# Gathers of a selective scan: 24 to 32 of a block's 64 taken from VectorE to ScalarE and GpSimd, with a convolution tap, an affine step and sums

## What is computed

```python
h = relu(adj @ x @ gcn_w + gcn_b)
h = (h - mu) * rsqrt(var + EPS) * ln_g + ln_b
xc, z = split(h @ w_in)
xconv = sum(xpad[k:k + L] * conv_w[:, k] for k in range(4)) + conv_b
u = silu(xconv)
dbc = u @ w_xp                       # 16 columns for dt, 16 for B, 16 for C
dt = softplus(dbc[:, :16] @ w_dt + b_dt)
hst = exp(dt * A) * hst + dt * B * u   # in time order, 512 channels x 16 states
ys = hst @ Ct
y = (ys + u * D_skip) * silu(z)
x = x + y @ w_out
```

## Time and profile before

| what | value |
|---|---|
| median of 3 runs (lowest, highest) | 2886.9 us (2885.34, 2891.23) |
| the profiled execution | 2887.87 us, span 2885.8 us |
| busy in the span | PE 87%, DVE 73%, ACT 47%, POOL 33% |
| chain that ended last | PE 51%, DVE 27%, issue 14%, ACT 6%, POOL 1% |
| mean granted TensorE clock | 0.937 of 2.4 GHz |
| first and last scan starts | 1336.7 and 2601.3 us |

### The profile page before, as it was taken

How to read it: one execution, slowest core, us unless ns; L and a number is a source line. 1 busy time by engine, 2 the same in 40 slices (tenths; PEclk the granted TensorE clock), 3 DMA queues, 4 the chain that set the end, 5 groups by cost and what they waited for, 6 DMA issues and landing times.

```text
span 2885.8 us, 24290 instructions
## 1 busy us (share of the span) xinstructions
PE 2505.6 (87%) x8262; PEld 1277.1 (44%) x8262; DVE 2119.0 (73%) x2426; ACT 1348.4 (47%) x1935; POOL 961.7 (33%) x723
## 2 busy tenths in 40 slices
PE   7998999999999999988888888888888876765997
PEld 3443444444444444443434343434434343443775
DVE  4665666666667664326999899999999999895564
ACT  4565656565646553214444434434353444552332
POOL 0002232313131313304455554645455464670000
PEclk9998999999999999999999999998999978777999
DMA  4222222222222231123323232322323110102021
GB/s 177 91 88 66 66 83 65 79 71 71 77 73 68 71 104 43 51 83 111 94 83 103 73 109 73 102 80 88 99 84 105 56 50 16 51 31 95 30 66 37
DMA packets 68412, 221.03 MB, mean 77 GB/s; under 512 B 7570, under 2 KB 7826, under 8 KB 67906
## 3 DMA queue, kind: packets, MB, share of 16 engines
q1 hardware_dynamic: 64082, 204.00, 22.4%
q0 software_dynamic: 3664, 14.45, 1.3%
q10 hardware_dynamic: 544, 1.05, 0.1%
HBM read 199.28 MB, written 20.19 MB: 76 GB/s over the span
## 4 chain that ended last, share of the span: by engine, by line
PE 51%; DVE 27%; issue 14%; ACT 6%; POOL 1%; DMA 1%; DVEq 0%; SPq 0%; ACTq 0%; POOLq 0%
PE ps L535 13%; DVE h L1265 9%; DVE acc L1239 7%; PE ps L558 5%; ACT th L1432 2%; PE ps L807 2%; PE ps L654 2%; PE ps L686 2%; PE ps L585 2%; PE ps L587 1%; PE ps L621 1%; PE ps L638 1%; PE ps L643 1%; DVE u L1182 1%; DVE wgt L966 1%
## 5 line engine op out<-in xcount | busy, mean ns | idle before, releaser
L1935 POOL TENSOR_TENSOR dB<-du,bc 128x512 f32<-128x512 f32 x512 | 649.3, 1273 | 559.2 <-DVE h L1265 556.4
L1265 DVE TENSOR_TENSOR_SCAN h<-ps,hst,dB 128x512 f32<-128x512 f32 x512 | 649.3, 1273 | 13.7 <-POOL dB L1935 6.6
L1432 ACT ACTIVATE ps<-dt,cols 128x512 f32<-128x512 f32 x512 | 350.9, 688 | 442.5 <-DVE h L1265 438.3
L535 PE MATMUL ps<-wgt,msg 128*128 128x512 f32 x1024 | 530.7, 621 | 23.0 <-DVE wgt L971 22.6
L558 PE MATMUL ps<-raw,msg 128*128 128x512 f32 x1024 | 543.4, 623 | 3.0 <-DMA msg<-tmp_m 3.0
L807 PE MATMUL ps<-consts,h 128*128 128x128 f32 x2048 | 353.5, 302 | 211.2 <-DVE acc L1239 196.9
L807 PEld LDWEIGHTS ps<-consts,h 128*128 128x128 f32 x2048 | 263.2, 153 | 531.9 <-DVE acc L1239 368.1
L1239 DVE SCALAR_TENSOR_TENSOR acc<-ps,Ct,acc 128x512 f32<-128x512 f32 x450 | 326.7, 726 | 8.9 <-PE ps L807 8.9
L535 PEld LDWEIGHTS ps<-wgt,msg 128*128 128x128 f32 x1024 | 184.2, 194 | 254.8 <-issue 200.7
L1432 ACT ACTIVATE wgt<-wgt 128x1024 f32<-128x1024 f32 x256 | 258.1, 1047 | 38.2 <-DVE wgt L966 35.7
L558 PEld LDWEIGHTS ps<-raw,msg 128*128 128x128 f32 x1024 | 176.5, 199 | 127.8 <-issue 127.0
(11 more groups left out here) (273 smaller groups left out, 3682.9 us busy)
## 6 DMA issues: line engine op xcount, KB each, us to landing
raw<-in_adjT SPq DMA_DIRECT2D x256, 512.0 KB, 3.6
bc<-tmp_bc SPq DMA_DIRECT2D x64, 512.0 KB, 4.8
xb<-in_xT POOLq DMA_DIRECT2D x8, 512.0 KB, 4.1
tmp_x<-xb POOLq DMA_DIRECT2D x8, 512.0 KB, 3.1
x<-tmp_x SPq DMA_DIRECT2D x8, 512.0 KB, 4.6
tmp_x<-x SPq DMA_DIRECT2D x8, 512.0 KB, 3.5
tmp_xn<-x SPq DMA_DIRECT2D x8, 512.0 KB, 3.6
raw<-tmp_xn SPq DMA_DIRECT2D x8, 512.0 KB, 4.1
```

Source lines behind the costliest of these rows:

```text
L535: x = e.matmul(P[d][:, :], msg[:, j, d * 128:(d + 1) * 128], wgt[g % NW][:, l, :], start=j == 0, stop=j == NJ - 1)
L1265: e.tensor_tensor_scan(hr[n % 3][:, m, :], PS[4 + k % 2].t[:, :], dBr[k % 4][:, :], hst[:, n % 16, m:m + 1], ALU.mult, ALU.add).then_inc(S ...
L1432: return e.activation(out, in_, func, bias=bias, scale=scale)
L1935: e.tensor_tensor(dBr[k % 4][:, :], du[:, m, :], bcr[i % 3][:, n % 2, :], ALU.mult).then_inc(S("dB"), 1)
```

## The change

Which engine adds a gather is now told by `adder(ib, n, s)`. For s = 0 the first state is a scaled copy by ScalarE straight into `acc`, and the 15 others are scaled by ScalarE into one of two buffers `part` and added to `acc` by GpSimd. For s = 1 GpSimd adds states 8 to 15 in blocks 0 to 5, and in blocks 6 and 7 TensorE sums all 16 as it did before for s = 0. All else is VectorE's. So 24 gathers leave VectorE in blocks 0 to 5, and 32 are off it in blocks 6 and 7, where 16 were before. `HANDED` numbers the 168 that GpSimd adds; it does so `HAND` = 10 units behind its products, ahead of the product of that unit. The gate transposes wait for the last of them.

Beside that: the tap on the newest column, with its bias, is made by ScalarE from the projection's bank straight into `u`, and VectorE adds three taps; the affine step after the norm goes to ScalarE; the inverse deviation stays in its PSUM bank (`norm_b`) and VectorE multiplies from there; the sums for the router are two accumulating copies on ScalarE.

```diff
-SHARED = {6: 1, 7: 1}
+HAND = LAG + 4
+
+
+def adder(ib, n, s):
+
+
+    if s == 0:
+        return "gpsimd" if n else "scalar"
+    if s == 1:
+        return "tensor" if ib >= NB - 2 else "gpsimd" if n >= 8 else "vector"
+    return "vector"
+
+
+def unit(j):
+
+    return j // 64, j % 64 // 4, j % 4
+
+
+
+HANDED = {j: i for i, j in enumerate(j for j in range(64 * NB) if adder(*unit(j)) == "gpsimd")}
...
+        part = [sb(cB, f"part{i}", [128, 512]) for i in range(2)]
...
-        r1 = sb(cB, "r1", [128, TB])
...
-                w.wait_ge(S("x3n"), ib + 1)
+                w.wait_ge(postb_use(ib, 3).evac, postb_use(ib, 3).n)
...
-                w.wait_ge(S("hbn"), 3 * ib + 3)
+                w.wait_ge(S("hba"), 2 * ib + 2)
...
-                    if ib in SHARED and s == SHARED[ib]:
+                    if s == 2 and adder(ib, n, 1) == "tensor":
...
-                            if s >= SHARED.get(ib, 0):
-                                last = hT_use(64 * ib + 60 + s)
+                            last, how = hT_use(64 * ib + 60 + s), adder(ib, 15, s)
+                            if how == "gpsimd":
+                                w.wait_ge(S("summed"), HANDED[64 * ib + 60 + s] + 1)
+                            elif how == "tensor":
+                                w.wait_ge(prod[0].use(2 * NB + ib - 6).evac, prod[0].use(2 * NB + ib - 6).n)
+                            else:
                                 w.wait_ge(last.evac, last.n)
...
-                w.wait_ge(S("rr1"), ib + 1)
-                e.tensor_tensor(hb[:, :, :], hb[:, :, :], two(r1), ALU.mult).then_inc(S("hbn"), 1)
-                w.wait_ge(S("hbn"), 3 * ib + 1)
-                for k in range(2):
-                    e.tensor_scalar(hb[:, k, :], hb[:, k, :], col("lng", k), col("lnb", k), ALU.mult, ALU.add).then_inc(S("hbn"), 1)
+                v = preb_use(ib, 1)
+                w.wait_ge(S("rr1"), 2 * ib + 2)
+                e.tensor_tensor(hb[:, :, :], hb[:, :, :], two(v.ps), ALU.mult).then_inc(v.evac, 1)
                 yield
                 n_th = 6 * ib
                 for m in range(4):
-                    b, c, at = preb_use(ib, 2 + 2 * m), u[p][:, m, :], 16 * ib + 4 * m
+                    b, c, at = preb_use(ib, 2 + 2 * m), u[p][:, m, :], 12 * ib + 3 * m
                     yield from (None, None, None)
+                    w.wait_ge(S("xcb"), 4 * ib + m + 1)
                     w.wait_ge(b.evac, b.n)
-                    e.tensor_scalar(c, xcb[:, m, 0:TB], col("cw1", 4 * m), col("cb1", m), ALU.mult, ALU.add).then_inc(S("conv1"), 1)
-                    for k in range(1, 4):
+                    for k in range(3):
...
-                w.wait_ge(S("rr3"), ib + 1)
-                e.tensor_tensor(x3[:, :, :], x3[:, :, :], two(r1), ALU.mult).then_inc(S("x3n"), 1)
-                w.wait_ge(S("x3n"), ib + 1)
-                e.tensor_reduce(sums[:, :, ib], x3[:, :, :], AX.X, ALU.add).then_inc(S("sum"), 1)
+                v = postb_use(ib, 3)
+                w.wait_ge(S("rr3"), 2 * ib + 2)
+                e.tensor_tensor(x3[:, :, :], x3[:, :, :], two(v.ps), ALU.mult).then_inc(v.evac, 1)
...
-                    if s >= SHARED.get(ib, 0):
+                    if adder(ib, n, s) == "vector":
...
+            def norm_b(xc_, sq_, m, v, squared, ln, n):
+
+                yield from (None, None, None)
+                w.wait_ge(m.evac, m.n)
+                act(sq_, xc_, ACT.Square).then_inc(squared, 1)
+                yield from (None, None, None)
+                w.wait_ge(v.full, v.n)
+                act(v.ps[:, :], v.ps[:, :], ACT.Ln, bias=EPS).then_inc(ln, 1)
+                w.wait_ge(ln, 2 * n - 1)
+                act(v.ps[:, :], v.ps[:, :], ACT.Exp, scale=-0.5).then_inc(ln, 1)
...
-                yield from norm(hb[:, :, :], sq1[:, :, :], r1[:, :], preb_use(ib, 0), preb_use(ib, 1), S("sq1"), S("rr1"))
+                yield from norm_b(hb[:, :, :], sq1[:, :, :], preb_use(ib, 0), preb_use(ib, 1), S("sq1"), S("rr1"), ib + 1)
+                v = preb_use(ib, 1)
+                w.wait_ge(v.evac, v.n)
+                for k in range(2):
+                    act(hb[:, k, :], hb[:, k, :], ACT.Identity, scale=col("lng", k), bias=col("lnb", k)).then_inc(S("hba"), 1)
...
-                    act(xcb[:, m, 3:TB + 3], b.ps[:, :], ACT.Identity).then_inc(b.evac, 1)
+                    act(xcb[:, m, 3:TB + 3], b.ps[:, :], ACT.Identity).then_inc(S("xcb"), 1)
+                    act(u[p][:, m, :], b.ps[:, :], ACT.Identity, scale=col("cw1", 4 * m + 3), bias=col("cb1", m)).then_inc(b.evac, 1)
...
-                yield from norm(x3[:, :, :], sq1[:, :, :], r1[:, :], postb_use(ib, 2), postb_use(ib, 3), S("sq3"), S("rr3"))
+                yield from norm_b(x3[:, :, :], sq1[:, :, :], postb_use(ib, 2), postb_use(ib, 3), S("sq3"), S("rr3"), ib + 1)
+                w.wait_ge(postb_use(ib, 3).evac, postb_use(ib, 3).n)
+                act(sq1[:, 0, :], x3[:, 0, :], ACT.Identity, accum=sums[:, 0, ib:ib + 1]).then_inc(S("sum0"), 1)
+                w.wait_ge(S("sum0"), ib + 1)
+                act(sq1[:, 0, :], x3[:, 1, :], ACT.Identity, accum=sums[:, 1, ib:ib + 1]).then_inc(S("sum"), 1)
...
-                    if s < SHARED.get(ib, 0):
-                        b = hT_use(j)
+                    b, c, how = hT_use(j), Ct[p][:, s, 32 + n:33 + n], adder(ib, n, s)
+                    if how != "vector":
                         w.wait_ge(b.full, b.n)
                         w.wait_ge(preb_use(ib, 15).evac, preb_use(ib, 15).n)
+                    if how == "scalar":
+                        if ib:
+                            w.wait_ge(gate_use(ib - 1, 3).full, gate_use(ib - 1, 3).n)
+                        act(acc[:, s, :], b.ps[:, :], ACT.Copy, scale=c).then_inc(b.evac, 1)
+                    elif how == "gpsimd":
+                        w.wait_ge(S("summed"), HANDED[j] - 1)
+                        act(part[HANDED[j] % 2][:, :], b.ps[:, :], ACT.Copy, scale=c).then_inc(b.evac, 1)
...
-                        act(raw[3][:, n % 2, :], b.ps[:, :], ACT.Copy, scale=Ct[p][:, s, 32 + n:33 + n]).then_inc(b.evac, 1)
-                    elif ib in SHARED and s == SHARED[ib] and n == 15:
+                        act(raw[3][:, n % 2, :], b.ps[:, :], ACT.Copy, scale=c).then_inc(b.evac, 1)
+                    elif s == 2 and n == 15 and adder(ib, n, 1) == "tensor":
...
-                        act(acc[:, 0, :], P[0][:, :], ACT.Identity).then_inc(f.evac, 1)
+                        act(acc[:, 1, :], P[0][:, :], ACT.Identity).then_inc(f.evac, 1)
...
-            for k in range(64 * NB):
+            def add(j):
+                ib, n, s = unit(j)
+                made, last = hT_use(j), hT_use(j - 4)
+                w.wait_ge(made.evac, made.n)
+                if j - 4 in HANDED:
+                    w.wait_ge(S("summed"), HANDED[j - 4] + 1)
+                else:
+                    w.wait_ge(last.evac, last.n)
+                e.tensor_tensor(acc[:, s, :], acc[:, s, :], part[HANDED[j] % 2][:, :], ALU.add).then_inc(S("summed"), 1)
+
+            for k in range(64 * NB + HAND):
+                if k - HAND in HANDED:
+                    add(k - HAND)
+                if k >= 64 * NB:
+                    continue
...
```

More of the change, by code:

```diff
@@ L327, in build @@
                   (gate_use(NB - 1, 3).full, gate_use(NB - 1, 3).n), (postb_use(NB - 1, 3).evac, postb_use(NB - 1, 3).n),
-                  (S("rr3"), NB), (S("gate"), 4 * NB), (S("d_x3s"), 16 * NB), (S("d_xn3"), 16 * NB), (S("d_bcs"), 16 * NB)]
+                  (S("rr3"), 2 * NB), (S("gate"), 4 * NB), (S("summed"), len(HANDED)), (S("d_x3s"), 16 * NB), (S("d_xn3"), 16 * NB), (S("d_bcs"), 16 * NB)]
         @block.sync
@@ L1450, in norm @@
                 yield from (None, None)
+            def norm_b(xc_, sq_, m, v, squared, ln, n):
[7 more added lines that the diff above has]
+                act(v.ps[:, :], v.ps[:, :], ACT.Exp, scale=-0.5).then_inc(ln, 1)
+                yield from (None, None)
             def messages(ib):
@@ L1659, in pre_b @@
                     if m % 2:
-                        w.wait_ge(S("conv1"), 16 * ib + 4 * m + 4)
+                        w.wait_ge(S("conv1"), 12 * ib + 3 * m + 3)
                         w.wait_ge(S("th1r"), n_th)
@@ L1668, in pre_b @@
                         yield
-                w.wait_ge(S("conv1"), 16 * ib + 16)
+                w.wait_ge(S("conv1"), 12 * ib + 12)
                 act(xcb[:, :, 0:3], xcb[:, :, TB:TB + 3], ACT.Identity).then_inc(S("halo1"), 1)
```

2 lines of the change are left out of this document (removed).

## The result

| | before | changed |
|---|---|---|
| median of the runs shown (us) | 2888.95 (2885.34 to 2891.23, 4 runs) | 2850.64 (2848.66 to 2854.16, 4 runs) |
| ratio, 95% interval | | 0.9869 [0.9854, 0.9884] |
| profiled execution, its span (us) | 2887.87, 2885.8 | 2851.44, 2849.3 |

Faster by 38 us, where 70 were forecast (2818). The time lies in the range, outside the forecast's own 2790 to 2845.

What follows compares the result with a forecast made beforehand. VectorE was taken to bound layer 1's scan. Blocks 1 to 5 gain 22.1 - 4.2 - 6.4 - 3 = 8.5 us each (42.5); with 7.3, 9.9 and 10.4 that makes 70 off 2887.9: 2818, range 2765 to 2872.

Steps and rivals of the forecast that it cites:

- The bound and what leaves: Layer 1's scan: VectorE bounds it, TensorE close behind; 22.1 us a block leave VectorE, other engines have room.
- One sign of being wrong: Named in advance: scans waiting for dB or an exponential for more than some 5 us a block.
- the 4 us of idle time before the gates: Sign of being right: some 4 us VectorE idle before a block's first gate, ended by TensorE, waiting for GpSimd's add.
- Tap, affine step, sums: Work leaving VectorE besides gathers: first tap 4.4 us a block, affine step and sums together 2.3.
- The gathers: Blocks 0 to 5 lose 24 of 64 gathers on VectorE, 0.64 us each: 15.4 us a block.
- First place: Block's end: gate transposes wait for GpSimd's last add; passage 26 us, giving back 4.2 in each of blocks 0 to 5.
- Collisions: VectorE instructions meeting GpSimd's at the ports: 22 exposed a block, 0.44 us each, 6.4 us a block more than before.
- Third, the queues in order: TensorE and ScalarE waiting in their in-order queues: 3 us a block lost, with nothing in the trace to price it.
- Blocks 0, 6, 7: Gains in the scan's blocks outside 1 to 5: 7.3 us in block 0, 9.9 in 6, 10.4 in 7.
- the queues lock: Rival: four engines wait for each other in turn, a third of the gain or less left: 2850 to 2887, chance 0.13.
- Cheap collisions: Rival: GpSimd's instructions fall mostly under scans and gathers, queues cost nothing; 134 us gained, 2753, chance 0.20.
- ports that make it slower: Rival: GpSimd becomes the bound through VectorE's ports, port waits 24.3 us a block; 60 slower, 2948, chance 0.09.

Runs made afterwards that it cites:

- moves_only: Changed kernel with the gathers left as before the change; only tap, affine step, norm from PSUM and sums moved: 2851.1 us, ratio 0.9869 to the kernel before.
- end_vector: Changed kernel with states 14 and 15 of the shared parts given back to VectorE, four gathers a block: 2831.25 us, ratio 0.9807 to the kernel before.
- early24: Changed kernel, but in blocks 0 to 5 the 24 handed gathers are states 0 to 11 of both shared parts: 2794.88 us, ratio 0.9676 to the kernel before.
- gathers_only: Changed kernel with norm, affine step, tap and sums as before the change; only the gathers moved: 2909.72 us, ratio 1.0086 to the kernel before.
- early16: Changed kernel, but only states 0 to 7 of both shared parts leave VectorE, 16 gathers a block: 2816.0 us, ratio 0.975 to the kernel before.

## Why the prediction was right, and where it was wrong

- **The bound and what leaves.** Right: VectorE's instructions are what the change removed, no engine took its place. GpSimd busy 114 of 158 is 118 a block (116 forecast), ScalarE 87 of 158 (90 of 157). VectorE's share is 0.849, where "still above 0.85" was to be seen; the period 163.0, where 158 was right and over 163 was wrong: on the edge. One sign of being wrong came: scans wait 8.3 us a block for dB and exponentials, where more than some 5 was named. Of the 4 us of idle time before the gates 2.1 came there, and 2.7 a little earlier, for dB.
- **Tap, affine step, sums: 6.7 us a block.** Right: moves_only gains 5.2, the rest lost to dearer taps (table: instructions 156.8 to 151.5).
- **The gathers: 15.4 us a block.** Wrong in their worth. Counted as instructions they are gone; in time they bring nothing (2850.6 with them, 2851.1 without), and alone they cost 22.
- **First place, 4.2 us.** The mechanism is shown by end_vector. The size: the passage was forecast at 26.0 and took 27.6, so 5.8 were given back. Of the 1.6 missed, 1.3 is GpSimd's late start behind the product that the dt step held up; 0.5 is the transposes at 1.1 where 0.6 stood, 0.2 the gates' products, less 0.4 for fifteen instructions that took 18.9 and not 19.3.
- **Collisions, 6.4 us.** Right in kind, too large: 3.3. The taps' mean of 1.2 us came true (1169 ns), and the gates' products went from 692 to 865 ns over the stage; but the dt step took 1312 ns where 0.44 us more were charged for each, the sz step lost nothing, and the silu step on u fell from 1790 to 1513.
- **Third, the queues in order: 3 us.** This step failed. Idle time grew by 15.6; less 4.7 in the passage (waits for dB and for the transposes) leaves 10.9, where 3 stood. "Nothing in the trace prices this" was not so: the earlier trace rows has VectorE waiting 1.22 us for th at a dt step. This is the end of a chain that VectorE's gathers covered almost to its end, and a gather taken out ahead of the first dt step only makes the wait longer: early24 has two fewer there and the same 17.3 us. (The waits for th at sz in the earlier trace rows are no such end: their chain starts with VectorE's own step on u, and they took 18.9 us in both kernels.) Besides, the handed copies stand in the way of the chain: from the first dt step to the second the changed kernel takes 13.8 us, moves_only 10.0. The trace shows ScalarE's copy late, TensorE waiting for it, dt's product behind that wait, and in three of four blocks the lower clock; no run tells these parts from one another. Of the 10.9 us, 8.0 are at the dt steps and 2.9 in the long stretch ahead. A removal of 15.4 us was priced as work on the bounding engine everywhere, though a bounding engine with short waits is bound only between them.
- **Blocks 0, 6, 7: 7.3, 9.9, 10.4.** Block 6 and 7 held (8.5, 10.8); there the last shared part goes over TensorE and, in block 7, no dt chain runs, but no run tells which of this it was. Block 0 gained nothing: ahead of its gates stand a scan that waits 4.0 us for an exponential, a dt step that waits 3.5, and then the passage.
- **The time.** About half of the forecast's 70 us came. In the account a block gains 22.1 - 4.7 - 3.3 - 10.9 = 3.2 us where 8.5 stood. That 2850.6 lies in the range is in part luck: the queues took 8 us a block more than was put down, and collisions that were put 3 us too dear made up for some of it.
- **Rivals.** Nearest is "the queues lock" (2850 to 2887), in time, where 2850.6 is its edge, and in part in kind: engines do wait for each other in turn at the dt steps and before the gates. TensorE's busy time did not change; where others wait for it, it has itself waited for ScalarE's copy or GpSimd's add. Cheap collisions (2753) and ports that make it slower (2948) did not happen; gathers_only is slower, but by 22 and by idle time, not by the 24.3 us of port waits a block. The Trainium skill (GPSIMD Engine Reference, opening) calls GpSimd the wrong choice for elementwise work. The runs agree so far that 168 adds cost 49 us; but early24, with 154 of them, is 56 us faster than the changed kernel.

What stays open: why early16 and early24 idle 4.7 and 6.5 us a block more than moves_only, most of it in the stretch before the second sz step; how much of the loss between the dt steps is queue order and how much the clock; and what the distance does to early24. A version with all early gathers handed over is the best found, 2793.8 to 2794.9, 3.2% under the kernel before.

## What to carry to other kernels

Before moving work off the engine that bounds a stage, look at what stands where that work is: beside another engine's chain of fixed length it is cover, and taking it away lengthens the wait by the same amount. Then look at the queue that the moved piece enters: a copy handed to ScalarE behind dt's functions held TensorE for 2.65 us, and dt's next product with it. Choose which of many equal pieces to move by their place, not by their number; here that was 56 us of 2850. Work that is handed through a shared queue should have no piece near a point where all engines meet: four gathers given back there were worth 19 us.
